# GpSimd's wait for the next tile of x, moved behind the two low-part subtractions

## The reference

```python
# layer 0: a 32x32 channel mix per batch entry (weights from an MLP on cond), then a linear
# layer with a rank-8 LoRA of the best of 4 experts
y  = einsum('boi,bih->boh', agg_w, x) + agg_b[:, :, None]
x1 = x + y @ W_up.T + delta0(y)          # delta0: top-1 expert
# layer 1: a grouped convolution over the width (9 taps, 4 groups), then a linear layer
# with a rank-16 LoRA of the best 2 of 8 experts
c   = conv_general_dilated(x1, weight, padding=[(4, 4)], feature_group_count=4) + ctx + bias
out = x1 + c @ W_base.T + b_base + delta1(c)
```

## Time and profile before

| what | value |
|---|---|
| median of 3 runs | 408.29 us (407.73 to 410.41) |
| profiled execution | 406.51 us |
| its span in the trace | 404.7 us, mean granted TensorE clock 0.992 |
| busy: PE, PEld, DVE, ACT, POOL | 356.3, 342.7, 237.6, 135.3, 200.5 us |

### The profile page before, as it was taken

One profiled execution on the slowest core, in us unless ns is written; L12 is line 12 of the kernel. 1 busy time (PEld: TensorE's weight loads), 2 busy tenths in 40 slices (PEclk: granted clock), 3 DMA queues, 4 the chain that ended last, 5 costly groups with the idle time before them and its releaser, 6 DMA issues.

```text
span 404.7 us, 9092 instructions
## 1 busy us (share of the span) xinstructions
PE 356.3 (88%) x2593; PEld 342.7 (85%) x2593; DVE 237.6 (59%) x977; ACT 135.3 (33%) x410; POOL 200.5 (50%) x229
## 2 busy tenths in 40 slices
PE   2878998689999999999998989898998999999985
PEld 1666998689998988898998989888998889898984
DVE  2667576256565655556566565556666565555654
ACT  2544333123333333332333333332333333333331
POOL 8476455424554455444455455444455455544540
PEclk9998999899999999999999999999999999999999
DMA  7524367333323223333322323333322323333221
GB/s 169 174 69 114 66 162 143 68 81 78 55 50 71 70 66 78 78 78 78 78 39 63 73 64 74 78 78 78 78 43 59 72 67 72 78 78 78 55 53 53
DMA packets 54301, 31.98 MB, mean 79 GB/s; under 512 B 43868, under 2 KB 44300, under 8 KB 54288
## 3 DMA queue, kind: packets, MB, share of 16 engines
q1 hardware_dynamic: 40064, 27.69, 28.7%
q10 hardware_dynamic: 13984, 3.73, 6.6%
q0 software_dynamic: 240, 0.41, 0.4%
HBM read 14.35 MB, written 8.93 MB: 58 GB/s over the span
## 4 chain that ended last, share of the span: by engine, by line
SPq 22%; DMA 21%; PE 15%; DVE 13%; issue 11%; POOL 6%; ACT 2%; ACTq 1%; DVEq 1%; POOLq 1%
SPq L294 21%; DMA xt<-in_x 18%; PE ps_mix L939 5%; POOL xq_lo L454 5%; DVE ps_ct L752 5%; PE ps_conv L939 4%; DVE x1s L725 4%; DMA xq<-x1s 2%; PE ps_up L917 2%; DVE zT L732 2%; ACTq L294 1%; DMA mix_all<-agg_mix 1%; PE ps_up L922 1%; SPq L301 1%; PE ps_base L1078 1%
## 5 line engine op out<-in xcount | busy, mean ns | idle before, releaser
L473 POOL TENSOR_TENSOR y_lo<-y,y_hi 128x512 fp32r<-128x512 f32 x31 | 40.0, 1291 | 102.5 <-ACT y_hi L527 102.5
L454 POOL TENSOR_TENSOR xq_lo<-xq,xq_hi 128x260 fp32r<-128x260 f32 x64 | 45.8, 735 | 82.4 <-DMA xt<-in_x 75.4
L1078 PE MATMUL ps_base<-base_hi,c_hi 128*128 128x392 f32 (+1 forms) x256 | 78.2, 322 | 1.8 <-ACT c_hi L573 1.3
L917 PE MATMUL ps_up<-up_hi,y_hi 128*128 128x292 f32 (+1 forms) x256 | 71.8, 304 | 4.6 <-DMA mix_all<-agg_mix 4.6
L1078 PE MATMUL ps_base<-base_lo,c_hi 128*128 128x392 f32 (+1 forms) x256 | 75.3, 311 | 0.0
L917 PE MATMUL ps_up<-up_lo,y_hi 128*128 128x292 f32 (+1 forms) x256 | 69.5, 293 | 0.0
L461 POOL TENSOR_TENSOR x1b<-x1s,bbase_s 128x256 f32<-128x256 f32 x64 | 57.7, 930 | 0.0
L917 PEld LDWEIGHTS ps_up<-up_hi,y_hi 128*128 128x128 f32 x256 | 49.0, 191 | 5.5 <-issue 5.5
L1078 PEld LDWEIGHTS ps_base<-base_hi,c_hi 128*128 128x128 f32 x256 | 48.2, 188 | 2.3 <-DVE ot L760 2.2
L917 PEld LDWEIGHTS ps_up<-up_lo,y_hi 128*128 128x128 f32 x256 | 49.1, 192 | 0.0
L1083 PE MATMUL ps_base<-base_hi,c_lo 128*128 128x392 f32 (+1 forms) x256 | 48.4, 311 | 0.0
(11 more groups left out here) (178 smaller groups left out, 669.9 us busy)
## 6 DMA issues: line engine op xcount, KB each, us to landing
xt<-in_x SPq DMA_DIRECT2D x32, 256.0 KB, 2.8
out_x<-ot SPq DMA_DIRECT2D x32, 256.0 KB, 2.7
xq<-x1s SPq DMA_DIRECT2D x160, 32.5 KB, 2.1
xq<-x1s ACTq DMA_DIRECT2D x96, 32.5 KB, 2.2
rows<-agg_rows SPq DMA_DIRECT2D x2, 597.0 KB, 5.0
wbase_raw<-in_L_ffn_W_base SPq DMA_DIRECT2D x2, 512.0 KB, 4.2
rows<-agg_rows SPq DMA_DIRECT2D x1, 598.0 KB, 4.4
wup_raw<-in_L_ffn_W_up ACTq DMA_DIRECT2D x2, 256.0 KB, 4.6
```

The costliest lines, as they stand in the source:

```text
L454: pool.tensor_tensor(xq_lo[:, gp], xq[:, gp], xq_hi[:, gp], ALU.subtract)\
L473: pool.tensor_tensor(y_lo[:], y32[:], y_hi[:], ALU.subtract).then_inc(ylo_done, 1)
L917: pe.matmul(into, y_hi[:, k], w[:, k, cols], start=(k == 0 and w is up_hi), stop=False, skip_group_check=True)
L1078: pe.matmul(ps_base[:, j, 0:width], c_hi[:, q], w[:, q, j, 0:width], start=(q == 0 and w is base_hi), stop=False, skip_group_check=True)
```

## The change

In GpSimd's body the wait for x of tile i+1 moves from the head of the body to a place behind the two xq_lo instructions, in front of the waits for x1b. The load of x, on SyncE's queue, stays where it is; so does every other instruction.

```diff
@@ gpsimd, body(i, par)
                 if once(i - 1):
 
-                    if once(i + 1):
-                        pool.wait_ge(x_in[1 - par], (i + par) * 8 + 16)
                     for gp in range(GP):
                         pool.wait_ge(xqhi_done, 2 * i - 1 + gp)
                         pool.wait_ge(xq_in[gp], i * XQ)
                         pool.tensor_tensor(xq_lo[:, gp], xq[:, gp], xq_hi[:, gp], ALU.subtract)\
                             .then_inc(xqlo_done, 1)
                     if isinstance(i, int) and i == 1:
                         pool.wait_ge(in_rows, 32)
+                    if once(i + 1):
+                        pool.wait_ge(x_in[1 - par], (i + par) * 8 + 16)
                     pool.wait_ge(x1_done, 2 * i)
                     after(pool, out_done, (i - 2) * 2)
                     for j in range(2):
```

## The result

The changed kernel takes 376.85 us (median of 4 runs, 375.75 to 377.56), the kernel before 408.01 us (median of 4, 406.51 to 410.41). The ratio is 0.923, 95% interval 0.918 to 0.928. The profiled execution took 377.56 us against 406.51, 28.95 less; its span is 375.8 us against 404.7.

A forecast was written before the change was run, and what follows sets the result against it. In mid-kernel TensorE was taken to be working or waiting for xq_lo, which GpSimd's wait for x held up. Removing 28 waits, 29.9 us, with no cost for xq_lo, contention or clock: 408.29 - 29.9 = 378.4 us; range 375.5 to 386.

The forecast's parts named there:

- What bounds the kernel: In the middle of the kernel TensorE is either working or waiting for xq_lo, held by GpSimd's wait for x; 1.08 us a tile.
- The gap closes wholly: Both xq_lo, freed of the wait for x, are hidden, so TensorE's idle gap of 1.08 us a tile goes.
- The sum: TensorE's weight loads stop waiting for xq_lo 28 times, saving 29.9 us; bounds 23.4 and 32.7 us.
- xq_lo's slack of 0.75 us: The second xq_lo ends at about T+6.35 (T: x1 complete), and TensorE wants it at T+7.1 for ps_mix.
- x1b: On GpSimd, now behind the wait for x, it ends at T+8.75; VectorE's x1_sum is due at T+9.4, slack 0.65 us.
- Contention: Both xq_lo now run beside VectorE's gate arithmetic; cost taken as nothing, at most 0.07 us on the one that counts.
- The tenth on x1b: GpSimd's x1b took 1.84 us in the loop against 1.68 where VectorE was idle, read as something paid for contention.
- The signs: Profile after: x1b waits 0.2 to 0.7 us for x, TensorE's xq_lo wait near zero, bodies 10.24 us apart, PE busy 95%.
- (a): The wait passes to the second half's xq, returning 0.17 us a tile if a microsecond later; 382.8 to 386 us, chance 0.18.
- (b): xq_lo was held by something else landing at the same time as x, so no gain; 408 us, chance 0.03.
- (c): x1b comes under x, delaying x1_sum and T; slower than before once x lands after T+8.6, some 416 us; chance 0.02.

The follow-up runs named there:

- experiment 1: Also called x_load_first: the kernel before, GpSimd's wait at its old place, but SyncE issues the load of x ahead of its five xq DMAs; 378.45 us.
- wait_between: The changed kernel, with GpSimd's wait for x placed between the two xq_lo instructions; 383.68 us.
- split_6_2: The changed kernel with GpSimd's wait moved behind x1b, and SyncE issuing six of eight xq DMAs, ScalarE two, instead of five and three; 378.21 us.
- split_7_1: The changed kernel with GpSimd's wait moved behind x1b, and SyncE issuing seven of eight xq DMAs, ScalarE one, instead of five and three; 395.82 us.
- late_x: The changed kernel, with the load of x issued behind the same body's output store and a wait for its landing; 414.47 us, ratio 1.016.
- mix_all_early: The changed kernel, with all four DMAs of the mix_all table issued in SyncE's body 2, instead of two each in bodies 2 and 3; 371.72 us.

## Why the prediction was right

*What bounds the kernel.* Right, and shown by experiment 1: with x early and the old order, the time is the same. TensorE works without a pause from 90 to 340 us, in that kernel as in the changed one.

*The gap closes wholly.* Right. 1.08 us a tile were predicted, 11.32 - 10.22 = 1.10 measured. The clean body of the earlier trace rows had 10.14, so a body of the loop is 0.08 longer than it.

*The sum.* 29.9 us predicted, 28.9 in the spans. The y_lo of body 4 starts at 85.21 before and 85.14 after, so up to there nothing was gained, though bodies 2 and 3 did gain: their share, 1.3 us, is given back by a later start of body 0 in this execution (y_lo at 36.28 against 35.07). From body 4's y_lo to body 5's 1.5 us are gained, in the next 24 bodies 26.6, at the end 0.7. The median moved by 31.2 us, more than either. The runs of before spread over 3.9 us, and their profiled execution, from which the 29.9 come, was the fastest of them. The median lies 1.5 us from the forecast of 378.4, within that spread; the rows of the loop test the sum more sharply than the medians do.

*xq_lo's slack of 0.75 us.* Right within its use: the second one was ready 0.86 us before TensorE's weight load (211.00 against 211.86), wait_between lost 0.2 us a body where 0.25 was expected from it, split_6_2 nothing, split_7_1 0.5.

*x1b.* Its slack was 0.65 us in the text and 0.8 in the trace for the later x: the two instructions end at 223.52, x1_sum starts at 224.35.

```profile
221.75 1.77 POOL L461 TENSOR_TENSOR x1b<-x1s,bbase_s 128x256 f32<-128x256 f32 x2 [0.49 <-DMA xt<-in_x]
...
224.35 0.75 DVE L725 TENSOR_TENSOR x1s<-ps_up,xtp 128x256 f32<-128x256 f32 x2
```

*Contention.* xq_lo's median went from 734 to 744 ns, now that it runs beside VectorE's gate arithmetic: 0.01 us, far under the slack. The Trainium skill's rule (page "GPSIMD Engine Reference", section "1. Specifications") would have had nothing there; the trace has a hundredth, which changes no term. The tenth on x1b is there after the change too: 1.66 us where VectorE stood idle (from 72.37), 1.77 and 1.78 in the loop. No run here shows what makes it.

*The signs.* The wait in front of x1b is there, 7.6 us in 24 waits and none over 0.6, where 0.2 to 0.7 us each were forecast. PE is busy 93% of the span and not 95%: the forecast kept its busy time of 356.3 us, and that fell to 351.3. What shortened it is not shown.

*The rivals.* (a) did not come about by itself, and split_7_1 shows that it is real once the second xq_hi comes 1.2 us later. (b) is out by experiment 1. (c) is real too: late_x is it, and its point lies where the text put it. There a landing at T+8.6 was to give the old distance of the bodies, 11.32 us, and each microsecond behind it one more; a landing at T+8.7 gave 11.46. The kernel is 1.6% slower than before.

## What to carry to other kernels

An in-order queue passes a wait on to everything behind it. Put each wait directly in front of the first instruction that reads the data, and behind everything that another engine is waiting for. When the wait is moved, name what stands behind it now and how long that may wait: in front of x1b the load of x had 0.8 us to spare, behind x1b at least the 2 us that were tried, at the same speed today. And when one engine becomes the bound over the whole loop, what is left is in its start and its end: look there for the next stop.

## What I had not expected of the hardware

The transfers were shorter where they did not overlap, which I had not allowed for. In late_x, where the store of the output and the load of x follow each other, their medians from issue to landing are 2.0 and 2.6 us; in the changed kernel, where they overlap, 2.6 and 2.8. This is a part of why x landed at T+8.7 and not at T+10, and late x cost half of my estimate. The time of an issue varies too: 0.35 us for x in x_load_first, 0.57 to 0.79 for each xq in late_x. The second half of xq came 0.27 us later with the load of x ahead of it, where I had counted a whole 0.65.

A stop of TensorE cost more than its length. The 4.4 us wait for the table in body 4 is gone in mix_all_early, and bodies 3 and 4 together are 6.2 us shorter. The chain that ended last in the changed kernel (start us, us, what) shows the rest:

```profile
70.11 4.16 DMA mix_all<-agg_mix
...
74.61 1.88 PE ps_up L917 x8
76.49 0.97 PE ps_up L922 x4
77.47 0.85 PE ps_conv L939 x4
...
78.82 0.72 PE ps_mix L939 x6
...
86.65 1.08 PE ps_up L917 x8
87.73 0.54 PE ps_up L922 x4
88.27 0.48 PE ps_conv L939 x4
...
89.10 0.72 PE ps_mix L939 x6
```

From the first up-projection matmul to the first of ps_mix it is 4.21 us just behind the wait (74.61 to 78.82) and 2.45 us a body later (86.65 to 89.10), with the same matmuls in both. The granted clock from 75.2 to 78.0 us is 0.50, which is 1.2 GHz, the lower of the two levels, after TensorE had stood still for 4.4 us; mix_all_early has 1.00 from 60 to 80 us. The slower matmuls cost 1.8 us, and 4.4 + 1.8 = 6.2 us is what the two bodies gained.
